# Receiver terms one chunk ahead, in quarters over five PSUM banks, in the second layer of a graph network

## The reference

```
sender_features   = nodes[src];  receiver_features = nodes[dst]
h   = relu(concat([sender, receiver, edge_attr_32]) @ W1 + b1)      # 200000 x 128
agg = segment_sum(h @ W2 + b2, dst) / max(degree, 1)
x   = layernorm(x + agg + nodes @ Wn + bn)
```

## Time and profile before

| | |
|---|---|
| median of three runs | 5320.2 us (5318.58 to 5334.47) |
| the profiled execution, its own time | 5303.53 us |
| its span, first to last instruction | 5301.8 us |
| layer 1's chunk loop (first gather to last row copy) | about 2774.8 to 5119 us |
| busy in the span | POOL 66%, DVE 41%, PE 33%, ACT 33% |
| mean granted TensorE clock | 0.608 of full speed |

### The profile page before, as it was taken

How to read it: one execution, slowest core, us unless ns; L and a number is a source line. 1 busy time by engine, 2 the same in 40 slices (tenths; PEclk the granted TensorE clock), 3 DMA queues, 4 the chain that set the end, 5 groups by cost and what they waited for, 6 DMA issues and landing times.

```text
span 5301.8 us, 22035 instructions
## 1 busy us (share of the span) xinstructions
PE 1752.7 (33%) x3727; PEld 739.0 (14%) x3747; DVE 2196.3 (41%) x2960; ACT 1728.1 (33%) x1393; POOL 3508.6 (66%) x3562
## 2 busy tenths in 40 slices
PE   4630000000000000003464455454555555555544
PEld 2210000000000000002231111111111111111113
DVE  3453222222222222225543465454555555455445
ACT  2422111111111111112233454454554555445431
POOL 5567777777777777775547566666666666666634
PEclk7965555555555555555556677676766767677665
DMA  4025333333333333332333344444444444444432
GB/s 165 7 79 170 107 107 107 107 107 107 106 107 107 106 107 106 107 102 85 98 104 116 120 160 140 135 151 133 153 151 140 146 151 152 133 152 150 134 104 79
DMA packets 202250, 635.79 MB, mean 120 GB/s; under 512 B 70347, under 2 KB 72848, under 8 KB 157808
## 3 DMA queue, kind: packets, MB, share of 16 engines
q1 hardware_dynamic: 88624, 457.72, 23.2%
q0 software_dynamic: 113344, 177.81, 14.3%
q10 hardware_dynamic: 256, 0.00, 0.0%
HBM read 335.07 MB, written 300.32 MB: 120 GB/s over the span
## 4 chain that ended last, share of the span: by engine, by line
POOL 29%; another core or an unknown queue 22%; issue 21%; DVE 15%; PE 10%; ACT 1%; DMA 1%; DVEq 1%; ACTq 0%; SPq 0%; POOLq 0%
POOL edge_arena L499 28%; DVE node_arena L1330 11%; PE ps L644 10%; POOL edge_arena L511 1%; ACT node_arena L822 1%; DVE edge_arena L1363 0%; DVE node_arena L1348 0%; DVE ps L1227 0%; POOL edge_arena L597 0%; DVE node_arena L1340 0%; DMA table<-node_arena 0%; DVE node_arena L1228 0%; DMA node_arena<-recv_term 0%; DVE node_arena L1224 0%
## 5 line engine op out<-in xcount | busy, mean ns | idle before, releaser
L597 POOL DMA_INDIRECT edge_arena<-table1s,ix x1568 | 1482.3, 945 | 816.4 <-issue 507.3
L499 POOL DMA_INDIRECT edge_arena<-table,ix x1440 | 1496.8, 1039 | 498.6 <-issue 498.6
L1330 DVE TENSOR_TENSOR_SCAN node_arena<-ps,node_arena 128x510 f32<-128x510 f32 (+1 forms) x980 | 945.5, 1038 | 97.2 <-issue 73.3
L644 PE MATMUL ps<-node_arena,ident 128*128 128x512 f32 x784 | 741.4, 1102 | 356.6 <-issue 247.8
L644 PE MATMUL ps<-w1e_bd,edge_terms 128*128 128x512 f32 x784 | 496.6, 782 | 760.7 <-issue 436.2
L644 PE MATMUL ps<-we_bd,edge_terms 128*128 128x32 f32 x392 | 93.6, 403 | 1885.1 <-issue 1495.1
L1363 DVE TENSOR_TENSOR edge_arena<-edge_arena,ps 128x1024 f32<-128x1024 f32 x196 | 238.6, 1218 | 1001.1 <-remote 806.2
L1170 DVE TENSOR_TENSOR score<-edge_arena,node_wide 128x128 f32<-128x128 f32 x49 | 18.6, 380 | 1466.6 <-DMA edge_arena<-table,ix 1451.0
L951 ACT ACTIVATE node_arena<-edge_arena 128x2048 f32<-128x2048 f32 x98 | 374.6, 3822 | 676.4 <-issue 670.5
L930 ACT ACTIVATE node_arena<-node_arena 128x2048 f32<-128x2048 f32 x98 | 375.3, 3830 | 523.3 <-DMA node_arena<-recv_term 450.7
L834 ACT ACTIVATE ps<-expo 128x128 f32<-128x128 f32 x49 | 13.8, 281 | 1402.8 <-issue 1244.6
(11 more groups left out here) (199 smaller groups left out, 1845.9 us busy)
## 6 DMA issues: line engine op xcount, KB each, us to landing
recv_term<-zeros SPq DMA_DIRECT2D x98, 1024.0 KB
node_arena<-recv_term SPq DMA_DIRECT2D x98, 1024.0 KB
rows<-edge_arena SPq DMA_DIRECT2D x98, 1024.0 KB
rows<-edge_arena SPq DMA_DIRECT2D x49, 1152.0 KB
edge_arena<-table,ix POOLq DMA_INDIRECT x1568
edge_terms<-e32g_d SPq DMA_DIRECT2D x98, 256.0 KB
edge_arena<-table1s,ix POOLq DMA_INDIRECT x1568
edge_terms<-e16g_d SPq DMA_DIRECT2D x49, 256.0 KB
```

What stands on the lines that cost most here:

```text
L499: pool.indirect_dma_start(G0[slot][:, u, :], None, table0, bass.IndirectOffsetOnAxis(ap=ix[slot][:, u:u + 1], axis=0)).then_inc(gathered0[ ...
L597: pool.indirect_dma_start(G1[slot][:, u, :], None, table1s, bass.IndirectOffsetOnAxis(ap=ix[slot][:, u:u + 1], axis=0)).then_inc(gathered1 ...
L644: return pe.matmul(out_, lhsT, rhs, start=start, stop=stop)
L1330: last = scan(F[:, lo:hi], hold[:, 0:hi - lo], F[:, lo:hi], 0.0, ALU.mult, ALU.add)
```

## The change

The scan of the receivers runs one chunk ahead, the PSUM banks are used by quarters of a chunk in a ring of five, the multiplier has three banks, and PE, ACT and DVE loops are written out. Cut to its core:

```
-        hold1 = [ps[:, r, 0:FEATS * T1] for r in range(2)]
+        HOLDS = 3
+        SUMS = 8 - HOLDS
+        QT = C1 // 4
+        hold1 = [ps[:, r, 0:FEATS * T1] for r in range(HOLDS)]
 SP, chunk c:
-                    sp.wait_ge(xf_ready, c + 1);  load X1 with chunk c + 1
-                    sp.wait_ge(edge1_mm, c * 2 + 4);  load edge features;  store1(c - 1)
+                    sp.wait_ge(xf_ready, c + 2);  load X1 with chunk c + 2
+                    store1(c - 1);  sp.wait_ge(edge1_mm, c * 4 + 4);  load edge features
 PE:
+            def edge1(c):
+                pe.wait_ge(e32_in[c % RING1], 16 * (c // RING1) + 16)
+                for g in range(4):
+                    n = 4 * c + g
+                    bank = ps[:, HOLDS + n % SUMS, :]
+                    if n >= SUMS:
+                        pe.wait_ge(added, n - SUMS + 1)
+                    mm(bank, edge_terms[c % RING1][:, g, :], w1e_bd[:, :], True, False)
+                    if g == 0:
+                        pe.wait_ge(scanned_x, c + 1)
+                    recv = F1_f[XF1[c % 2]][:, :, 1 + QT * g:1 + QT * g + QT]
+                    mm(bank.rearrange("p (t f) -> p f t", f=HID), ident[:, :], recv, False, True).then_inc(edge1_mm, 1)
+            for c in range(K1):
+                edge1(c)
 ACT:
+            def turn1(c):
+                if c:
+                    rows_1(c - 1)
+                if HOLDS <= c + 2 < K1:
+                    hold_1(c + 2)
+                if c + 2 < K1:
+                    act.wait_ge(edge1_mm, 4 * c + 4)
+                    act.wait_ge(led_x, c + 2)
+                    recv_1(c + 2)
+                act.wait_ge(added, 4 * c + 4)
+                ...
+                act.activation(F1_f[HF1[c % 2]]..., G1[c % RING1], ACT.Relu).then_inc(relu_done, 1)
+                ...
+            for c in range(2):
+                recv_1(c)
+            for c in range(K1):
+                turn1(c)
 DVE:
+            def adds1(c):
+                dve.wait_ge(gathered1[c % RING1], (c // RING1 + 1) * (16 * C1))
+                for g in range(4):
+                    n = 4 * c + g
+                    pre = G1[c % RING1][:, QT * g:QT * g + QT, :].rearrange("p t f -> p (t f)")
+                    dve.wait_ge(edge1_mm, n + 1)
+                    tt(pre, pre, ps[:, HOLDS + n % SUMS, :], ALU.add).then_inc(added, 1)
+            receivers1(0)
+            for c in range(K1):
+                if c + 1 < K1:
+                    receivers1(c + 1)
+                if c:
+                    sums1(c - 1)
+                with_b2(c)
+                adds1(c)
```

More of the change, by code:

```diff
@@ L747, in _ @@
             pe.wait_ge(pds_out, NB // 2 + 2)
[L750 to L754, removed]
+            def edge1(c):
+                pe.wait_ge(e32_in[c % RING1], 16 * (c // RING1) + 16)
                 for g in range(4):
[L756 to L770, removed]
+                    n = 4 * c + g
[9 more added lines that the diff above has]
+                edge1(c)
             pe.wait_ge(rows1_ready, K1 + 1)
-            for h in range(2):
-                pe.wait_ge(half_used[h], K1 + 1)
+            pe.wait_ge(added, 4 * K1)
             mm(ps[:, 0, 0:P], H1[(K1 - 1) % 2][:, C1 - 1, :], same_segT[:, :]).then_inc(carry1_mm, 1)
@@ L937, in turn1 @@
[L937 to L949, removed]
+                act.wait_ge(rows1_stored[c % 2], 16 * (c // 2) + 16)
@@ L955, in _ @@
             act.wait_ge(arena_free, 1)
[L956 to L965, removed]
+            for c in range(HOLDS):
+                hold_1(c)
@@ L1000, in _ @@
             dve.sem_inc(pds_out, 2)
-            for h in range(2):
-                dve.sem_inc(half_used[h], 1)
             dve.sem_inc(agg_used, 1)
@@ L1319, in with_b2 @@
                 stt(own, row_bc[:, 2, :], has[:, bass.ds(col, 1)], own, ALU.mult, ALU.add)
-            dve.memset(hold1_f[0][:, :, 0:1], 0.0)
-            link(dve.memset(hold1_f[1][:, :, 0:1], 0.0))
+            for h in hold1_f:
+                last = dve.memset(h[:, :, 0:1], 0.0)
+            link(last)
             dve.sem_inc(rows1_ready, 1)
@@ L1352, in turn1, with sums1 @@
                 dve.wait_ge(hold1_ready, c + 1)
-                if first:
-                    dve.memset(F1_f[HF1[1]][:, :, C1:T1], 0.0)
-                scan1(F1[XF1[r]], hold1[r], scanned_x)
-                if not first:
-                    sums1(c - 1, 1 - r)
-                with_b2(c)
-                dve.wait_ge(gathered1[s], it * (16 * C1) + 16 * C1)
-                for h in range(2):
-                    pre = G1[s][:, 8 * h:8 * h + 8, :].rearrange("p t f -> p (t f)")
-                    dve.wait_ge(edge1_mm, c * 2 + (h + 3))
-                    tt(pre, pre, ps[:, 2 + 2 * h:4 + 2 * h, :].rearrange("p a b -> p (a b)"), ALU.add).then_inc(half_used[h], 1)
-            turn1(0, 0, 0, first=True)
-            with dve.Fori(0, K1 // RING1) as it:
-                for i in range(RING1):
-                    turn1(it * RING1 + (i + 1), (i + 1) % RING1, it + (i + 1) // RING1)
-            turn1(K1 - 1, (K1 - 1) % RING1, (K1 - 1) // RING1)
+                scan1(F1[XF1[c % 2]], hold1[c % HOLDS], scanned_x)
+            def sums1(c):
+                dve.wait_ge(scanned1, c + 1)
+                dve.tensor_copy(F1_f[HF1[c % 2]][:, :, 0:1], F1_f[HF1[1 - c % 2]][:, :, C1:T1]).then_inc(led_h, 1)
+                dve.wait_ge(led_h, c + 1)
+                dve.wait_ge(relu_done, c + 1)
+                scan1(F1[HF1[c % 2]], hold1[c % HOLDS], scanned1)
+            def adds1(c):
[6 more added lines that the diff above has]
+            receivers1(0)
+            dve.memset(F1_f[HF1[1]][:, :, C1:T1], 0.0)
+            for c in range(K1):
+                if c + 1 < K1:
+                    receivers1(c + 1)
+                if c:
+                    sums1(c - 1)
+                with_b2(c)
+                adds1(c)
             for col in range(K1, NB):
                 with_b2(col)
-            lead1(K1 - 1, (K1 - 1) % 2)
-            sums1(K1 - 1, (K1 - 1) % 2)
+            sums1(K1 - 1)
             dve.wait_ge(rg0_in[0], 16 * NB // 2)
```

53 lines of the change are left out of this document (24 added, 29 removed).

## The result

In alternate runs on one chip the changed kernel takes 5371.7 us (median of 5, 5352.07 to 5376.07), the kernel before 5318.6 (median of 5, 5306.98 to 5334.47): ratio 1.0088, 95% interval 1.0058 to 1.0119. In a later series of runs the ratio was 1.0077 (1.0050 to 1.0104). The prediction was 5285 us and faster; the time is inside the range, the sign is wrong.

What follows compares the result with a forecast made beforehand. POOL's gathers (20.0 us a chunk) plus pauses from late completions bound the loop; 0.35 us less a chunk, other terms 0, gave own time 5268.5, plus 16.7 for the runs' median: 5285 us, range 4950 to 5420.

Steps and rivals of the forecast that it cites:

- The bound: Layer 1's loop: POOL's gathers 20.0 us a chunk plus pauses; matmul completions late at 2.75 us a row while gathers run.
- SP: The store moves ahead of the wait for `edge1_mm`; ACT's wait there holds back receiver copy and ReLU; priced at 0.
- The pause term of the sum: POOL's pauses: 12 us could serve four chunks instead of 10.9 three; 0.35 us less a chunk, 34 us over 98.
- The ring: ACT and DVE: rows copy, multiplier, receiver copy and ten scans take 18.9 us a chunk, hidden below POOL's 20.0.
- rival of 5467: ACT's order decides: late chunk every third at 37.4 us, others 18.9, so 147 us more; chance 0.12.
- Scan ahead: PE no longer waits for its own chunk's scan: at most 3.8 us in a fast chunk, little expected overall.
- the fifth bank: PSUM: lets PE issue one quarter before the first add of the chunk ahead; no separate size given.
- Quarters: DVE: four adds of 512 elements for two of 1024, taken as 2.7 us beside ACT's copies, so 0.
- Identity matmuls: PE: new read in runs of four and stepped write, 0.95 us a row (bounds 0.45 to 2.0), PE not the limit.
- rival of 5595: The PSUM write makes PE the bound: 2.85 us an identity row, 26.4 a chunk, 274 us more; chance 0.08.
- Loops written out: Register steps go, more instructions are fetched: bounds -29 to +196 us, taken as 0.
- The late completions go: Rival: POOL runs without pauses, 358 us less in the loop, 4958 us in all; chance 0.15.

Runs made afterwards that it cites:

- b4: The kernel before with each edge and identity matmul cut in two of 256 columns, 32 rows a chunk: 5505.0 us, ratio 1.0343.
- b2: The kernel before with eight of a chunk's sixteen gathers left out: 4495.3 us, 15.46 us a chunk.
- a6: The changed kernel with eight of a chunk's sixteen gathers left out: 4762.7 us, 18.11 us a chunk.
- d1: The kernel before without identity matmuls, VectorE adding the receiver terms to the PSUM banks in place: 5155.7 us, ratio 0.9672.
- c1: The changed kernel with a third receiver buffer: 5309.9 us, ratio 0.9968 to the kernel before.
- c3: The changed kernel with a third receiver buffer and ScalarE's old order: 5282.2 us, ratio 0.9910 to the kernel before.
- a1: The changed kernel with ScalarE's old order, in the short condition: ratio 1.0005 to the kernel before.
- a2: The changed kernel with the identity matmuls' old read and write, in the short condition: ratio 1.0001 to the kernel before.
- c4: The kernel before without identity matmuls, VectorE adding receiver terms to gathered ones, 8 rows a chunk: 5216.4 us, ratio 0.9798.

## Why the prediction was wrong, step by step

- *The bound.* Late completions at 2.75 us a row and POOL's pauses were read rightly (by its own rows they are 18 and 23 us late, not 15 to 23); `b4` shows the pace by rows (2.80), `b2` and `a6` that the lateness goes with half the gathers, `d1` that half the rows, with the add on VectorE, pay 3.3%. Wrong was POOL's 20.0 us as its share in a sustained loop: 16 x 1.39 = 22.2 is what layer 0 and `d1` show in the long condition, and if that holds in this loop too, before's 23.8 had 1.6 us above it, not 3.8. Layer 0's row would have told.
- *The step that failed* stands under SP: "In ACT the wait for `edge1_mm` now holds back `recv_1` and the ReLU behind it; that ReLU needs the adds of the same chunk anyway." The wait is indeed shared, but the copy's own time then lies between the late step and the ReLU on which POOL's next gather hangs: 2.94 of its 3.83 us, for which the sum had no term. Taking the copy off this path (`c1`) gives 1.1 to 1.2%, and the change with it is 0.3% faster than before (0.9968).
- *The pause term of the sum*, -0.35 us a chunk, lay between 10.9 us per three chunks and 12 per four. It was 21.3 per five (4.36 + 15.73 beyond the 0.30, and 1.2 in the gap behind the long pause), 4.3 a chunk: with 20.0 that is the 24.3 of the cycle. In `c1` it is 18.4 per five. The 10.9 per three also came from a stretch with single late chunks, and a third of before's cycles have two. With the copy off the path the forecast's sign and half its size come out (-0.3% for -0.7%).
- *The ring.* Fast chunks are 18.1 us, forecast 18.9; it alone sets the pace in `a6`. The sum had it at nothing, as hidden under POOL's 20.0, but in `c3` its removal is worth 0.6%: the second term that failed, half the size of the first. The rival of 5467 (every third chunk late at 37.4, the others 18.9) did not come: late chunks are no more frequent than before, 32 of 89 for 36.
- *Scan ahead* and *the fifth bank*: not tried alone. *Quarters*: 4 x 0.68 = 2.7 us, as taken; what they cost or bring was not tried alone. *Identity matmuls*: 0.90 us a row for 0.95 in the mean, but that mixes 0.50 at full and 0.86 at half clock; PE no bound; the rival of 5595 is out. *Loops written out*: not tried alone; in the short condition the variants `a1` and `a2`, which have them, are within 0.15% of before, so there fetching costs nothing that shows.
- *The late completions go* (4958): they did not; the change keeps 16 rows a chunk. In the short condition, where none is late, the kernel before takes 4572.

Open: what holds completions back. That gathers issued at 1.25 us and drained at 1.39 build a backlog, and completions are late while it lasts, fits `b2`, `a6` and `c4` (22.7 us a chunk, nothing late), but was tested by no run. One row's 2.80 us are two gathers of 1.40; whether that is more than a coincidence no run tells. Open too are why `c1`'s long pause did not shrink, and what makes the long and the short condition.

## To carry to other kernels

When an instruction is moved ahead of another and the two wait for the same event, the wait is shared but its own duration is not: it is added to every path through the second, less what runs beside it (here 2.94 of 3.83 us). Price it where that event comes last, and give it an older event to wait for (a third buffer) before changing the order. And take an engine's pitch from a stretch long enough that its queue is full, in another stage if need be.

## What the runs showed of the hardware

- The same program took 5320 or 4573 us from series to series; long rows of gathers (layer 0) ran at 1.39 or 1.25 us each, and matmul completions were some 20 us late or not at all.
- In the long condition completions came at 2.80 us a row, for rows of 512 and of 256 columns alike.
- A write to PSUM with a step of 128 elements, with a read in runs of four, took 0.50 us a row of 512 columns at full clock, a straight row 0.43, and a straight write with a read of step 17 took 0.90 (`a1`, `a2`). The Trainium skill, Advanced Engine Details and Errata, PSUM Cachelines, says that any non-contiguous pattern slows matmuls significantly; here it is at most 0.07 us a row, and the measurement decides for this pattern.
- At half clock the same rows took 0.86 and, with the strided read, 0.91 us: the new pattern went with the clock, the strided read did not.
- A VectorE add of 3.78 us with two SBUF operands held a gather for 4.33 us (2.8 us more than 0.94 in the mean of 97); with one operand and the result in PSUM (3.79 us), the gathers beside it kept 0.94 to 0.96 early in the loop of `d1`.
